# Lightning attention on one core: states ahead of the second decay, and the last gates computed block by block

## The reference

```python
xn = _layernorm(x)                                    # x: 4 x 512 x 512
# lightning attention over (2, 1024, 512), 16 heads of 128
qkv = silu(einsum('bnf,of->bno', xn, w_qkv)); q, k, v = split(qkv)
# over blocks: out = (q * q_decay) @ kv + ((q @ k.T) * diag_decay) @ v
#              kv  = block_decay * kv + (k * k_decay).T @ v
out = norm_w * out * rsqrt(mean(out * out) + 1e-6)
s = (sigmoid(einsum('bnf,of->bno', xn, w_gate)) * out) @ w_out.T
# ffn: softmax router over 64 experts, top 8, weighted sum of expert biases
f = xn * sum(topk_w) + einsum('tk,tkh->th', topk_w, expert_bias[topk_idx])
return x + s * silu(f)
```

## Time and profile before

| | |
|---|---|
| median of 3 runs | 1179.84 us (1179.35 to 1181.41) |
| the profiled execution's own time | 1181.1 us |
| its span | 1179.3 us |
| PE busy | 1104.1 us, 94% of the span |
| DVE, POOL, ACT busy | 625.4, 570.1, 508.3 us |
| mean granted TensorE clock | 0.99 |

### The profile page before, as it was taken

One profiled execution on the slowest core, in us unless ns is written; L12 is line 12 of the kernel. 1 busy time (PEld: TensorE's weight loads), 2 busy tenths in 40 slices (PEclk: granted clock), 3 DMA queues, 4 the chain that ended last, 5 costly groups with the idle time before them and its releaser, 6 DMA issues.

```text
span 1179.3 us, 17081 instructions
## 1 busy us (share of the span) xinstructions
PE 1104.1 (94%) x6546; PEld 967.2 (82%) x6546; DVE 625.4 (53%) x1080; ACT 508.3 (43%) x813; POOL 570.1 (48%) x450
## 2 busy tenths in 40 slices
PE   5998999999999999999999899999999999999985
PEld 4987879798887979888797787988888798888874
DVE  6653454535545453566547545454454545455766
ACT  5644353443525344452553525334352533545242
POOL 4554454454446444453627636445453643526244
PEclk9998999999999999999999999999999999999998
DMA  6262111101111110112814111011111111010021
GB/s 238 85 242 67 36 36 48 43 19 54 36 37 36 54 37 19 36 55 72 303 37 143 42 49 36 21 53 35 37 42 48 36 32 53 25 36 19 36 72 72
DMA packets 28079, 73.10 MB, mean 62 GB/s; under 512 B 3040, under 2 KB 3168, under 8 KB 28000
## 3 DMA queue, kind: packets, MB, share of 16 engines
q1 hardware_dynamic: 28000, 72.02, 18.6%
HBM read 59.43 MB, written 12.58 MB: 61 GB/s over the span
## 4 chain that ended last, share of the span: by engine, by line
PE 84%; DVE 9%; ACT 3%; issue 3%; POOL 1%; DMA 1%; POOLq 0%; SPq 0%; DVEq 0%; ACTq 0%
PE st_ps L464 11%; PE st_ps L466 10%; PE st_ps L465 10%; PE head_ps L606 5%; PE score_ps L580 5%; PE out_ps L616 5%; PE v_ps L554 5%; PE v_ps L556 5%; PE v_ps L555 5%; PE out_ps L617 5%; PE out_ps L618 5%; DVE q_t L1568 4%; PE head_ps L609 3%; PE tk_ps L591 2%; PE tk_ps L572 2%
## 5 line engine op out<-in xcount | busy, mean ns | idle before, releaser
L464 PE MATMUL st_ps<-xt_hi,w_hi 128*128 128x512 f32 x630 | 260.2, 413 | 22.2 <-DVE q_t L1517 22.2
L466 PE MATMUL st_ps<-xt_hi,w_lo 128*128 128x512 f32 x630 | 248.4, 394 | 0.0
L465 PE MATMUL st_ps<-xt_lo,w_hi 128*128 128x512 f32 x630 | 247.3, 393 | 0.0
L1289 POOL TENSOR_TENSOR w_lo<-land_a,w_hi 128x768 fp32r<-128x768 f32 x45 | 82.8, 1839 | 238.6 <-ACT w_hi L917 238.6
L1602 DVE TENSOR_TENSOR acc<-acc,out_ps 128x512 f32<-128x512 f32 x120 | 82.4, 687 | 210.6 <-PE out_ps L618 210.4
L1307 POOL TENSOR_TENSOR w_lo<-land_a,w_hi 128x1024 fp32r<-128x1024 f32 x45 | 112.2, 2494 | 104.1 <-ACT w_hi L922 104.1
L464 PEld LDWEIGHTS st_ps<-xt_hi,w_hi 128*128 128x128 f32 x630 | 119.8, 190 | 45.4 <-DVE q_t L1517 24.9
L466 PEld LDWEIGHTS st_ps<-xt_hi,w_lo 128*128 128x128 f32 x630 | 119.1, 189 | 26.6
L465 PEld LDWEIGHTS st_ps<-xt_lo,w_hi 128*128 128x128 f32 x630 | 119.9, 190 | 20.8
L554 PE MATMUL v_ps<-wv_hi,xt_hi 128*128 128x256 f32 (+1 forms) x472 | 135.8, 288 | 0.0
L556 PE MATMUL v_ps<-wv_hi,xt_lo 128*128 128x256 f32 (+1 forms) x472 | 134.3, 285 | 0.0
(11 more groups left out here) (295 smaller groups left out, 2225.2 us busy)
## 6 DMA issues: line engine op xcount, KB each, us to landing
land_a<-wgrp_dram SPq DMA_DIRECT2D x48, 512.0 KB, 3.6
land_b<-wv_dram SPq DMA_DIRECT2D x16, 512.0 KB, 3.6
land_b<-wo_dram SPq DMA_DIRECT2D x16, 512.0 KB, 3.6
xt_hi<-spill_hi SPq DMA_DIRECT2D x16, 256.0 KB, 5.1
xt_lo<-spill_lo SPq DMA_DIRECT2D x16, 256.0 KB, 6.7
out_dram<-acc SPq DMA_DIRECT2D x16, 256.0 KB, 2.0
spill_hi<-gate_hi SPq DMA_DIRECT2D x11, 256.0 KB, 2.0
spill_lo<-gate_lo SPq DMA_DIRECT2D x11, 256.0 KB, 2.5
```

The costliest lines, as they stand in the source:

```text
L464: pe.matmul(ps[:, :], w_h2, x_h2, start=first and k == 0, stop=False, skip_group_check=True)
L465: pe.matmul(ps[:, :], w_h2, x_l2, start=False, stop=False, skip_group_check=True)
L466: end = pe.matmul(ps[:, :], w_l2, x_h2, start=False, stop=last and k == 1, skip_group_check=True)
L1289: pool.tensor_tensor(flat(w_lo[:, buf, 0:3, :, :]), flat(land_a[:, 0:3, :, :]), flat(w_hi[:, buf, 0:3, :, :]).bitcast(F32), ALU.subtract). ...
```

## The change

It has five parts, and the computed result is the same.

1. DVE, every step 1 to 14, `GATE` group: `query_decay(1,0)` and `gate_low(0,0)` stand ahead of `score_decay(1,1)`, and `states(1,0)` ahead of `query_decay(1,1)`. In step 8 `sum0(7)` moves with them, ahead of `score_decay(1,1)`.
2. Step 0: the direct blocks go round three banks at first, so block 2 waits for no bank, and blocks 3 and 4 for an older one.
3. Step 1, ACT and POOL: `raw_hi` of the `QK1` weights, which needs a transfer, goes behind the decays, the squares and `act_c22`; `out_hi` goes ahead of `act_c21`. On POOL `mask_decay` and `add_square` go ahead of `raw_lo`.
4. Step 15: `GATE` is not made by seven products but by four direct blocks of 12 matmuls (48 for 42), without sums of weights and without joins; ACT takes each block straight from PSUM. Heads, ffn rows and output rows stand between the blocks.
5. The tail: sums of squares and norm in two halves, one for each sequence; `acc` is scaled on ACT and gets its residual on POOL (`add_x`), while DVE weighs the output rows by norm and ffn row in one operation (`weigh_last`) and adds (`join_last`).

```diff
@@ direct blocks
+        def direct_bank(j):
+            return st_ps[j] if j < 3 else st_ps[(j + (j < 12)) % 2]
...
-                n, buf, ps = j // 4, j // 4 % 2, st_ps[j % 2]
-                if j >= 2:
-                    pe.wait_ge(acted, j - 1)
+                n, buf, ps = j // 4, j // 4 % 2, direct_bank(j)
+                if n == FINAL:
+                    pe.wait_ge(acted, 4 * (n - 1) + A_C21 if j % 4 < 2 else j - 1)
+                elif j >= 3:
+                    pe.wait_ge(acted, j - 2 if j < 5 else j - 1)
@@ ACT, step
                 take_square(before, 0, 1)
-                raw_hi(group(ss, QK1), buf[1])
+                if ss > 1:
+                    raw_hi(group(ss, QK1), buf[1])
                 decays(ss, odd)
                 act.preload_act_table(ACT.Silu)
                 act_c11(ss, QK0)
+                take_square(before, 1, 0)
                 if ss == 1:
...
                     gate_high(0, 0, 0)
-                take_square(before, 1, 0)
                 gate_high(before, 1, 0)
                 act_c22(ss, QK0)
+                if ss == 1:
+                    raw_hi(group(ss, QK1), buf[1])
+                    out_hi(0, 0)
                 act_c21(ss, QK0)
                 take_square(before, 1, 1)
                 act_c12(ss, QK0)
-                if ss == 1:
-                    out_hi(0, 0)
                 sums_hi(group(ss, QK1), buf[1])
@@ DVE, step
                 e5(ss, GATE)
-                score_decay(ss, 1, 1)
                 if close:
                     sum0(7)
-                    scale0(6)
...
                 query_decay(ss, 1, 0)
                 gate_low(ss, 0, 0)
+                score_decay(ss, 1, 1)
+                if close:
+                    scale0(6)
+                states(ss, odd, 1, 0)
                 query_decay(ss, 1, 1)
-                states(ss, odd, 1, 0)
...
                 e7(ss, GATE)
                 gate_head(ss, 0, 1)
@@ PE, after the steps
+            direct_block(4 * FINAL)
+            head_output(LAST, 0, 0)
+            turn_and_score(LAST, 1, 0)
+            bias1(0)
+            bias1(1)
+            direct_block(4 * FINAL + 1)
+            pe.wait_ge(joined, joins(FINAL - 1) + E7)
+            head_output(LAST, 0, 1, ps=st_ps[2])
+            turn_and_score(LAST, 1, 1)
+            bias1(2)
+            bias1(3)
+            kv_products(1, LAST, 1, 0)
+            direct_block(4 * FINAL + 2)
+            head_output(LAST, 1, 0)
             kv_products(1, LAST, 1, 1)
+            bias1(4)
+            bias1(5)
+            pe.wait_ge(squared, 4 * LAST + 3)
+            pe.wait_ge(sq_added, 4 * LAST + 1)
+            pe.wait_ge(state_set, (NCH - 1) * (4 * LAST + 4))
+            sum_squares(0, tk_ps, square)
+            direct_block(4 * FINAL + 3)
...
+            last_rows(0)
+            head_output(LAST, 1, 1, ps=score_ps)
+            bias1(6)
+            bias1(7)
...
+            last_rows(1)
...
+            sum_squares(1, tk_ps, tail_square)
+            last_rows(2)
...
@@ ACT, end
+            root_rms(4, slice(NCH, TILES), tk_ps)
+            act.wait_ge(rms_step, 3 * RMS_STEPS)
+            for t in range(NCH, TILES):
+                scale_old(t)
@@ POOL, end
+            weigh(6)
+            weigh(7)
+            for t in range(2, TILES):
+                add_x(t)
@@ DVE, end
+            rms_scale(2, slice(NCH, TILES))
+            for t in range(2, TILES):
+                weigh_last(t)
+                join_last(t)
```

More of the change, by code:

```diff
@@ L610, in head_output, with last_rows @@
                 last.then_inc(head_full, 1)
+            def last_rows(i):
+                if i < NCH:
+                    output_rows(LAST, i, tail_out[i], gate_hi, gate_lo)
+                else:
+                    output_rows(LAST, i, tail_out[i], tail_gate_hi, tail_gate_lo)
             def output_rows(ss, i, ps, hi, lo):
@@ L839, in _ @@
+            sum_squares(0, tk_ps, square)
+            direct_block(4 * FINAL + 3)
             pe.wait_ge(gate_l, 4 * LAST + 3)
             pe.wait_ge(wo_l, LAST + 1)
-            for i in range(2):
-                output_rows(LAST, i, tail_out[i], gate_hi, gate_lo)
-            pe.wait_ge(squared, unit(LAST + 1, 0, 0))
-            pe.wait_ge(sq_added, unit(LAST, 1, 0))
-            sum_squares(0, score_ps, square)
-            output_rows(LAST, 2, tail_out[2], gate_hi, gate_lo)
-            sum_squares(1, score_ps, tail_square)
@@ L1092, in step @@
                 gate_high(before, 1, 1)
-                sums_hi(group(ss, GATE), buf[2])
+                if not final:
+                    sums_hi(group(ss, GATE), buf[2])
                 act_c11(ss, QK1)
@@ L1110, in step @@
                     act.preload_act_table(ACT.Silu)
-                if not final:
-                    raw_hi(group(ss + 1, QK0), buf[1])
+                raw_hi(group(ss + 1, QK0), buf[1])
                 if close:
@@ L1378, in step @@
                     finish0(1)
[L1379 to L1380 removed]
+                values_lo(ss + 1)
                 if close:
@@ L1385, in step @@
                     zero(1)
-                if not final:
-                    raw_lo(group(ss + 1, QK0), buf[1])
-                    weight_sums(group(ss + 1, QK0))
+                raw_lo(group(ss + 1, QK0), buf[1])
+                weight_sums(group(ss + 1, QK0))
                 if close:
@@ L1395, in step @@
                     add_square(bp, ss, 0, 0)
-                if final:
-                    for t in range(5):
-                        weigh(t)
-                if not final:
-                    sums_lo(group(ss + 1, QK0), buf[1])
+                sums_lo(group(ss + 1, QK0), buf[1])
                 if close:
@@ L1883, in _ @@
+            gate_head(LAST, 0, 0)
+            sum1(0)
+            sum1(1)
+            score_decay(LAST, 1, 0)
+            query_decay(LAST, 1, 0)
+            first_gate_low(0)
+            score_decay(LAST, 1, 1)
+            sum1(2)
+            sum1(3)
+            states(LAST, 1, 1, 0)
+            query_decay(LAST, 1, 1)
+            gate_head(LAST, 0, 1, ps=st_ps[2])
             states(LAST, 1, 1, 1)
-            gate_head(LAST, 1, 0, ps=st_ps[1])
+            gate_head(LAST, 1, 0)
             tail_gate_low(0)
+            sum1(4)
```

268 lines of the change are left out of this document (143 added, 125 removed).

## The result

The changed kernel took 1145.62 us (median of 4 runs, 1143.91 to 1146.48) against 1180.48 us (median of 4, with one run more than in the table ahead), a ratio of 0.970 with a 95% interval of 0.969 to 0.972: 34.9 us less. Its profiled execution took 1146.5 us, with a span of 1144.7.

The account below looks back on a forecast made before the run. PE, busy 94% of the span, was taken as the bound, so only its waits or the tail could give time. 16.6 + 3.5 + 1.0 + 5.2 + 2.8 + 6.8 = 35.9 us off 1181.1; forecast 1145, range 1136 to 1155.

Parts of the forecast that it names:

- Passages: Thirteen passages from step to step: DVE's work behind the held decay starts 1.28 us earlier, 16.6 us in all.
- e7: DVE operation in each passage, ahead of ACT's gate and `p6`: foretold at 1071.26 instead of 1072.54, 1.28 us earlier.
- The rival that DVE wins the port: Passages: second decay takes 0.55 us, PE waits for nothing; 2.57 us a passage, 33.4 not 16.6, time 1128; 7%.
- The clock: Behind two passages (165 and 729 us): shorter stalls regain most of the clock loss, 2.8 us, bounds 0 and 3.1.
- Step 8: Passage 8 to 9: the 2.76 us key-row wait goes, gaining 3.5 us; PE then waits 1.2 us before `p6`.
- The start: Parts 2 and 3: 1.0 us before direct block 2 and 5.2 in step 1, some from the clock; 6.2 together.
- both new waits: Step 1: 1.4 us before `turn_and_score`, and one before `output_tile(0)` for `out_lo`; about 1 us each in the trace.
- The tail: Parts 4 and 5, from the last group on: 6.8 us less, bounds 3 and 9.
- PE's one wait: Tail: `sum_squares(0)` waits for the square of head (1,0); PE idle 1.7 us.

Follow-up runs that it names:

- start_alone: The kernel before with parts 2 and 3 alone (banks of the direct blocks, order of ACT and POOL in step 1): 1175.03 us, ratio 0.995.
- states_only: The kernel before with one move: in steps 1 to 14 the states stand ahead of the second `query_decay`: 1175.51 us, ratio 0.996.
- gate_low_back: The changed kernel with the first `query_decay` and `gate_low` of steps 1 to 14 put back behind `probs`: 1164.61 us, ratio 0.985.
- late_decay: The changed kernel with the second `query_decay` of steps 1 to 14 moved into the next step on DVE, where `out_lo` has ended: 1120.66 us, ratio 0.949.

## Why the prediction was right, and where it was not

**Passages.** Foretold 1.28 us each, measured 1.27. The chain was as described: join, first decay, `gate_low`, `probs`, states, held decay, `e7` right behind `out_lo`. Its two terms show apart: 0.97 for the states (68.40 to 67.43) and 0.31 for `gate_low` (67.44 to 67.13). The forecast of 1.2 to 1.4 us before `p6` was low: it is 1.55. From the last product of `p3` to `p6`, waits left out, PE took 1.30 us before and 1.06 now that `kv_products` has no wait of its own, so PE comes to `p6` 0.24 us sooner than counted.

**The rival that DVE wins the port** had the cause right and too low a price. It had 2.57 us a passage; without the clash it is 3.20 (68.40 to 65.20), and 1121 us, not 1128. Three kernels show it, from DVE's side twice and from POOL's once. The Trainium skill (SBUF — State Buffer, Who interferes with whom) has issue order decide, and the runs agree: a decay that starts 0.72 us ahead of `out_lo` takes 0.55, one that starts 0.25 behind it takes 2.56.

**The clock** is the step where the reasoning failed though the number held (2.8; 2.7 in the ledger). It was argued that shorter waits can still be hit. Of single waits of 1.55 us before `p6`, none of 26 was followed by a drop, nor were the two of 1.21 in step 8; of 1.84 us, 16 of 26; of 0.87 and 1.70 with `kv_products` between them, 2 of 13 before and 11 of 52 over four kernels, 5 of these in the slowest execution of `start_alone`. A drop costs 1.5 us. The counts are of one profiled execution for each kernel, but the mean granted clocks of the others agree: 0.980 in all of `states_only`, 0.982 to 0.985 in `gate_low_back`, 0.995 to 0.998 in the changed kernel. So `gate_low`, which I priced at 0.32 us a passage, was worth 1.2, and without it the change would have come out at a ratio of 0.985, some 1163 us. The term was also too narrow: it counted the drops at 165 and 729 us and not the one at 650, and took back nothing for the tail. All in all the clock gave 1.4 + 1.3 + 1.6 in step 8 + 2.7 in step 1 and took 1.7 in the tail, some 5.3 us. That the sum came out at 34.9 for 35.9 owes something to luck: the clock's gain in step 8, which was in no term, stood against its loss in the tail. The Trainium skill (TensorE: Matmul & The Clock Gate, What's actually happening) ties the clock to how busy PE was recently; by that rule the work around a wait counts and not the wait alone. That the tail's wait of 1.44 us was followed by a drop and those of 1.55 were not agrees with it; that the pair of waits, longer in sum, was followed by fewer drops than the single one is not explained by it.

**Step 8.** The size was right (3.4 for 3.5), partly by luck. The wait of 1.2 us before `p6` came as foretold (1.21), but half of the 3.4 us is the clock drop at 650 us, which is in no term. And `sum0(7)` alone gives nothing that can be measured, since the pair of waits comes back in its place.

**The start.** 6.2 foretold, 6.1 measured, with both new waits at 1.38 and 0.80 us. Some of it was said to come from the clock; in step 1 that was more than half, 2.7 of 4.9 us. `out_lo` was held by its place on POOL behind a square: moved, the first tile no longer waited.

**The tail** was mis-sized: 6.8 foretold, 4.9 measured. PE's one wait was named (1.7 us, measured 1.44), but not what the clock does behind it: 1.7 us. Other errors cancelled. The second norm took 3.4 us on DVE instead of 1.1, three of its small steps held by POOL's operations; against that, the last join ended 9.6 us behind the norm and not 10.5, and the span 2.5 us behind the last join, not 3.9 (why the last store comes sooner was not tested). The prediction's own sum has a slip: 1157.0 + 10.8 is 1167.8, not 1168.5. Rows of the changed kernel:

```profile
1129.36 0.50 DVE L1514 TENSOR_TENSOR rms<-rms 128x4 f32<-128x4 f32 x1
1129.89 1.21 DVE L1516 TENSOR_TENSOR rms<-rms 128x4 f32<-128x4 f32 x1
1131.13 1.22 DVE L1518 TENSOR_SCALAR rms<-rms 128x4 f32<-128x4 f32 x1
1132.39 0.16 DVE L1520 TENSOR_TENSOR rms<-rms 128x4 f32<-128x4 f32 x1
...
1129.79 2.54 POOL L1492 TENSOR_TENSOR acc<-acc,tail_res 128x512 f32<-128x512 f32 x2
```

PE's last product starts 42.3 us after the group's first (1134.98 and 1092.65), where about 41 were foretold: the clock.

## What to carry to other kernels

Where one engine's operation is held by another's, look first at which of the two starts first, and by how much: moving work out from behind the held operation gave 1.3 us a step, moving the held operation 0.7 us ahead of the other, or behind its end, gave 3.2. Price a stall of PE at more than its idle time: 0.3 to 0.4 us on top for each restart in this kernel, and 1.5 us where the clock falls. A change that shortens a stall a little can be worth much more than it shortens (here 1.2 us for 0.3), or nothing, so read the granted clock behind each stall on both sides before adding up a ledger. When two moves are made together, run each alone: here one took away most of what the other had opened.

## What the runs showed of the hardware

- A wait costs PE more than the idle time that the profile shows. Step lengths without, with one wait of 1.55, with one of 1.84 and with two of 2.57 in sum are 65.20, 67.13, 67.44 and 68.40: each wait costs 0.3 to 0.4 us beside itself. Most of it can be seen in the rows: from `kv_products` to `p6` it is 2.38 us in the changed kernel (first two rows) and 0.58 in `late_decay` (last two), 1.80 us more for a wait of 1.55.

```profile
1043.26 0.83 PE L595 MATMUL tk_ps<-v_row,k_row 128*128 128x128 f32 x6
1045.64 0.50 PE L470 MATMUL st_ps<-xt_hi,w_hi 128*128 128x512 f32 x1 [1.55 <-DVE q_t L1582]
...
1019.52 0.83 PE L595 MATMUL tk_ps<-v_row,k_row 128*128 128x128 f32 x6
1020.10 0.48 PE L470 MATMUL st_ps<-xt_hi,w_hi 128*128 128x512 f32 x1
```

- Single waits of 1.55 us were followed by no drop of the clock (0 of 26) and those of 1.84 by one in 16 of 26. Yet a wait of 1.44 us, followed by sixteen one-column products instead of 512-column ones, was followed by a drop in the profiled execution of all six kernels that had it; it need not come each time, since two further runs of the changed kernel had a mean granted clock of 0.998 against 0.995. A wait of 3.6 us in step 1 was followed by a drop in three kernels of four, one of 2.76 us in step 8 likewise. So the length of a wait alone does not decide. That the narrow products are what made the difference was not tested, and why 10 of 26 equal waits were spared stays open.
- DVE's operations on 128x4 elements took 0.16 us each alone and 1.2 beside POOL's residual sums, TENSOR_SCALAR, which reads one tensor, among them: its row (1131.13 to 1132.35) ends with POOL's (1132.33). The exclusion is not one of large operations only.
